# Order of a fused decoder layer's operations, written out by hand, laid out anew on all four engines

## What is computed

```python
x = _layernorm(x + _L0_attn_ref(x, Wq, Wk, Wv, Wo))        # 16 heads of 128, 4 key/value heads, rope, softmax
x = _layernorm(x + _L0_xattn_ref(ctx, ctx, x, filt, D, 8)) # causal long convolution of k*v products, times q
x = _layernorm(x + _L0_ffn_ref(x, W_gate, W_qkv))          # top-1 gated key/value head, causal softmax attention
```

## Time and profile before

| | |
|---|---|
| median of 3 executions | 339.27 us (338.3 to 340.88) |
| profiled execution | 338.36 us, of which the profile's span is 336.5 us |
| PE busy | 312.7 us (93%) |
| DVE busy | 262.9 us (78%) |
| ACT busy | 231.3 us (69%) |
| POOL busy | 204.7 us (61%) |
| granted TensorE clock | 0.994 of full speed |

### The profile page before, as it was taken

How to read it: one execution, slowest core, us unless ns; L and a number is a source line. 1 busy time by engine, 2 the same in 40 slices (tenths; PEclk the granted TensorE clock), 3 DMA queues, 4 the chain that set the end, 5 groups by cost and what they waited for, 6 DMA issues and landing times.

```text
span 336.5 us, 6269 instructions
## 1 busy us (share of the span) xinstructions
PE 312.7 (93%) x2073; PEld 241.0 (72%) x2073; DVE 262.9 (78%) x502; ACT 231.3 (69%) x693; POOL 204.7 (61%) x289
## 2 busy tenths in 40 slices
PE   6889899999989979999999999999999999999982
PEld 2777678888879868878877977877566576656641
DVE  2776986857866884987697499998899899987656
ACT  3679477858858766867685677554477877777781
POOL 0598865737953827694892159995896876802022
PEclk9999999999999999999999999999999999999997
DMA  6940112010020311313000000000000000000001
GB/s 188 348 184 1 63 33 93 1 33 1 16 79 0 95 32 34 93 62 130 7 2 1 0 3 1 2 0 3 0 0 3 2 1 19 0 18 19 16 14 50
DMA packets 5760, 13.87 MB, mean 41 GB/s; under 512 B 864, under 2 KB 3040, under 8 KB 5472
## 3 DMA queue, kind: packets, MB, share of 16 engines
q1 hardware_dynamic: 5456, 13.08, 11.8%
q10 hardware_dynamic: 272, 0.39, 0.4%
HBM read 12.42 MB, written 1.05 MB: 40 GB/s over the span
## 4 chain that ended last, share of the span: by engine, by line
PE 36%; DVE 23%; issue 15%; POOL 14%; ACT 8%; DMA 3%; POOLq 0%; DVEq 0%; ACTq 0%
PE bank L401 5%; DVE q_rope L1607 5%; PE bank L548 5%; PE bank L423 4%; ACT prob L1163 4%; PE bank L438 4%; DVE t_cos L1594 2%; POOL kv L328 2%; PE bank L659 2%; PE bank L617 2%; POOL t_sin L2287 2%; DVE head_lo L1722 2%; PE bank L670 2%; POOL kv L331 2%; ACT rot L1128 2%
## 5 line engine op out<-in xcount | busy, mean ns | idle before, releaser
L2315 POOL TENSOR_TENSOR prob<-prob,rden 128x512 f32<-128x512 f32 x32 | 35.5, 1114 | 49.4 <-DVE rden L1680 49.4
L2287 POOL TENSOR_TENSOR t_sin<-rot,sin 128x512 f32<-128x512 f32 x36 | 47.3, 1324 | 29.8 <-ACT rot L1128 24.0
L1163 ACT ACTIVATE prob<-bank,neg_max 128x128 f32<-128x128 f32 x128 | 45.4, 376 | 14.2 <-DVE neg_max L1673 14.0
L548 PE MATMUL bank<-wo_hi,head_hi 128*128 128x256 f32 x128 | 38.6, 302 | 1.0 <-DVE head_lo L1722 1.0
L1243 ACT ACTIVATE prob<-bank,fneg_max 128x128 f32<-128x128 f32 x128 | 36.8, 383 | 2.3 <-DVE fneg_max L1837 2.2
L2352 POOL TENSOR_TENSOR rstd<-var_eps,half_pow 128x1 f32<-128x1 f32 (+1 forms) x18 | 11.1, 620 | 41.8 <-DVE var_eps L1762 41.0
L401 PE MATMUL bank<-x_hi,w_hi 128*128 128x512 f32 x96 | 33.0, 425 | 3.4 <-DVE w_hi L1641 1.5
L548 PE MATMUL bank<-wo_hi,head_lo 128*128 128x256 f32 x128 | 36.0, 281 | 0.0
L548 PE MATMUL bank<-wo_lo,head_hi 128*128 128x256 f32 x128 | 35.9, 281 | 0.0
L1607 DVE TENSOR_TENSOR q_rope<-t_cos,t_sin 128x512 f32<-128x512 f32 x28 | 33.4, 1214 | 1.8 <-POOL t_sin L2287 1.7
L1127 ACT COPY rot<-bank 64x512 f32<-64x512 f32 x40 | 23.4, 584 | 16.4 <-PE bank L401 13.7
(11 more groups left out here) (132 smaller groups left out, 812.0 us busy)
## 6 DMA issues: line engine op xcount, KB each, us to landing
w_raw<-in_wqkv SPq DMA_DIRECT2D x4, 768.0 KB, 4.3
toep<-in_toep SPq DMA_DIRECT2D x8, 256.0 KB, 3.1
wo_raw<-in_wo SPq DMA_DIRECT2D x4, 512.0 KB, 3.5
x_raw<-in_xt SPq DMA_DIRECT2D x2, 512.0 KB, 5.4
ctxT<-in_ctx SPq DMA_DIRECT2D x1, 1024.0 KB, 4.9
x<-in_x SPq DMA_DIRECT2D x1, 1024.0 KB, 9.0
out<-x SPq DMA_DIRECT2D x8, 128.0 KB, 1.7
wf<-in_wf SPq DMA_DIRECT2D x1, 784.0 KB, 4.3
```

Of the source, the lines that this page charges most:

```text
L548: last = pe.matmul(acc_bank[k // 2][:, (k % 2) * D:(k % 2 + 1) * D], hp[:, k % 2, h * P:(h + 1) * P], wp[:, g % 2, h, :], start=(h + n == ...
L1163: last = act.activation(prob[:, k % 2, h * P:(h + 1) * P], score_bank[k % 2][:, h * P:(h + 1) * P], ACT.Exp, bias=neg_max[:, k % 2, h:h + ...
L2287: pool.tensor_tensor(t_sin[:, par, :].rearrange("p (b t) -> p b t", b=BH), rot[:, par, :].rearrange("p (b t) -> p b t", b=BH), sin[:, :].u ...
L2315: pool.tensor_tensor(own, own, rden[:, k % 2, :].unsqueeze(2).to_broadcast([P, HG, P]), ALU.mult).then_inc(norm_done, 1)
```

## The change

No function is changed and no call is added or taken away; a line with four unused names is added. The lists of calls of TensorE, ScalarE, VectorE and GpSimd are permuted (477 lines out, 478 in). SyncE's list stays as it is. Cut to what the text below speaks of; the list is named ahead of each part by its hunk.

TensorE, the start, units 0 and 1, the entry to the third block, and the end:

```diff
@@ -730,172 +731,172 @@
             front_scores(0, range(0, 3))
+            front_scores(0, range(3, HG))
             v_turn(0)
-            front_scores(0, range(3, HG))
             front_scores(1, range(HG))
             item(0, "K")
             item(0, "Q0")
-            turn(0, 0)
             scores(0, 2)
             scores(0, 3)
+            turn(0, 0)
             item(0, "Q1")
+            item(0, "Q2")
+            values(0, 0)
             turn(0, 1)
-            values(0, 0)
-            item(0, "Q2")
+            conv(0, first_conv_bank, first_conv_done)
             item(0, "Q3")
+            output(0, 0)
+            values(0, 1)
             turn(0, 2)
-            conv(0, first_conv_bank, first_conv_done)
-            values(0, 1)
-            output(0, 0)
             item(0, "C1")
             item(0, "C2")
-            values(0, 2)
             output(0, 1)
             item(0, "C3")
+            values(0, 2)
+            turn(0, 3)
             scores(1, 0)
+            scores(1, 1)
+            values(0, 3)
+            output(0, 2)
             item(0, "C4")
...
             item(1, "Q2")
             item(1, "Q3")
-            turn(1, 2)
-            values(1, 1)
+            scores(1, 3)
+            item(1, "C5")
             output(1, 0)
-            item(1, "C5")
-            output(1, 1)
             item(1, "C6")
             item(1, "C7")
             item(1, "C8")
-            values(1, 2)
-            turn(1, 3)
-            scores(2, 0)
-            scores(2, 1)
+            values(1, 1)
+            turn(1, 2)
             item(1, "C9")
             item(1, "V")
+            turn(1, 3)
             item(2, "K")
             v_turn(2)
+            values(1, 2)
+            scores(2, 0)
...
             output(7, 3)
+            fscores(0, 0)
             x2_turn(1)
-            fscores(0, 0)
...
             fscores(7, 1)
+            fvalues(6, 3)
             fturn(7, 0)
-            fvalues(6, 3)
             fturn(7, 1)
+            y_turn(6)
             last_values(0)
             last_values(1)
             fturn(7, 2)
             fturn(7, 3)
             last_values(2)
-            y_turn(6)
             last_y_turn(0)
```

ScalarE, the start and the end:

```diff
@@ -1264,305 +1265,305 @@
             front_rotate("Q1")
-            split_x(1)
             front_rotate("Q2")
             front_rotate("Q3")
+            split_x(1)
             front_copy_vT()
+            split_wo(0)
             copy_v(0)
-            split_wo(0)
...
             fexps(7, 1)
-            fexps(7, 2)
+            yT_copy(6)
             fprob_copy(7, 0)
             fprob_copy(7, 1)
+            fexps(7, 2)
             fexps(7, 3)
             fprob_copy(7, 2)
-            yT_copy(6)
```

VectorE, the start with unit 0, the entry to the third block, and the end:

```diff
@@ -1889,376 +1890,376 @@
             first_w_high()
+            split_x(0)
             split_w(0, 0)
-            split_x(0)
             split_w(0, 1)
             front_cos_K()
+            front_cos("Q0")
             front_add_K()
-            front_cos("Q0")
             front_cos("Q1")
-            add_skip(0)
             front_cos("Q2")
+            front_cos("Q3")
             split_x(1)
-            front_cos("Q3")
             row_max(0, 0)
             value_low(0)
             row_max(0, 1)
+            front_add()
             invert(0, 0)
-            front_add()
+            add_skip(0)
             invert(0, 1)
             cos_item(0, "K")
             row_max(0, 2)
-            prob_low(0, 0)
-            invert(0, 2)
             cos_item(0, "Q0")
             add_item(0, "K")
+            invert(0, 2)
+            prob_low(0, 0)
+            row_max(0, 3)
             cos_item(0, "Q1")
+            head_low(0, 0)
             prob_low(0, 1)
-            head_low(0, 0)
             add_item(0, "Q0")
...
+            row_max(1, 1)
+            add_skip(1)
+            add_skip(2)
             split_w(1, 0)
...
             mix_norm(0)
+            first_apply(2)
+            prob_copy(7, 1)
             invert(7, 2)
-            second_apply(0)
-            prob_copy(7, 1)
             head_low(7, 0)
             row_max(7, 3)
-            prob_copy(7, 2)
             accumulate(6, 1)
+            second_apply(0)
...
             head_low(7, 3)
+            add_mix(1)
+            set_mask()
             mix_norm(1)
+            accumulate(7, 1)
             second_apply(1)
-            accumulate(7, 1)
...
+            y_invert(6)
             ffn_norm(5)
+            y_scale(6)
             ffn_apply(5)
+            ffn_norm(6)
             last_turn_copy()
-            y_invert(6)
-            y_scale(6)
+            ffn_apply(6)
             last_scale(0)
             last_scale(1)
-            ffn_norm(6)
             ffn_norm(7)
-            ffn_apply(6)
             ffn_apply(7)
```

GpSimd, the start of unit 0's part:

```diff
@@ -2360,91 +2361,91 @@
             normalize(0, 0)
-            normalize(0, 1)
             sin_item(0, "K")
             sin_item(0, "Q0")
+            normalize(0, 1)
+            split_wo(0)
+            sin_item(0, "Q1")
             normalize(0, 2)
-            sin_item(0, "Q1")
-            split_wo(0)
             sin_item(0, "Q2")
             sin_item(0, "Q3")
+            normalize(0, 3)
             pairs(1, range(0, 3))
             pairs(1, range(3, HD))
-            normalize(0, 3)
```

More of the change, by code:

```diff
@@ L810, in _ @@
             turn(2, 3)
-            output(2, 0)
+            scores(3, 0)
             item(2, "C14")
@@ L814, in _ @@
             scores(3, 1)
+            item(3, "K")
+            v_turn(3)
+            output(2, 2)
             scores(3, 2)
@@ L817, in _ @@
             turn(3, 0)
[L818 to L821, removed]
             item(3, "Q0")
-            turn(3, 1)
[L824 to L829, removed]
+            item(3, "Q1")
+            scores(3, 3)
+            item(3, "Q2")
+            item(3, "Q3")
+            values(3, 0)
+            turn(3, 1)
             output(2, 3)
             item(3, "C15")
+            output(3, 0)
             item(3, "C16")
             values(3, 1)
+            turn(3, 2)
             scores(4, 0)
-            output(3, 0)
+            item(3, "C17")
             output(3, 1)
-            item(3, "C17")
             item(3, "C18")
@@ L876, in _ @@
             turn(5, 0)
-            item(5, "K")
+            output(4, 2)
             scores(5, 2)
@@ L881, in _ @@
             values(5, 0)
+            turn(5, 1)
+            output(4, 3)
             item(5, "Q2")
             item(5, "Q3")
-            turn(5, 1)
-            output(4, 3)
+            turn(5, 2)
+            values(5, 1)
+            scores(5, 3)
+            item(5, "C26")
             output(5, 0)
-            scores(5, 3)
+            item(5, "C27")
+            output(5, 1)
             scores(6, 0)
[L889 to L892, removed]
             item(5, "C28")
@@ L1987, in _ @@
             invert(2, 3)
-            head_low(2, 1)
             prob_low(2, 2)
+            accumulate(1, 1)
+            split_w(2, 0)
+            add_skip(4)
             row_max(3, 0)
-            prob_low(2, 3)
-            accumulate(1, 1)
+            row_max(3, 1)
             head_low(2, 2)
             invert(3, 0)
-            row_max(3, 1)
+            value_low(3)
+            prob_low(2, 3)
             row_max(3, 2)
-            split_w(2, 0)
+            cos_item(3, "K")
+            split_w(2, 1)
@@ L1998, in _ @@
+            accumulate(2, 0)
+            add_item(3, "K")
             invert(3, 1)
-            invert(3, 2)
-            value_low(3)
-            split_w(2, 1)
+            cos_item(3, "Q0")
             head_low(2, 3)
+            cos_item(3, "Q1")
             prob_low(3, 0)
-            cos_item(3, "K")
-            cos_item(3, "Q0")
-            prob_low(3, 1)
-            add_item(3, "K")
             add_item(3, "Q0")
-            cos_item(3, "Q1")
-            head_low(3, 0)
-            add_skip(4)
@@ L2034, in _ @@
             cos_item(4, "K")
             add_item(4, "K")
+            cos_item(4, "Q0")
             prob_low(4, 0)
-            cos_item(4, "Q0")
+            cos_item(4, "Q1")
+            accumulate(3, 0)
+            add_skip(6)
             add_item(4, "Q0")
-            invert(4, 1)
-            invert(4, 2)
-            add_skip(5)
-            head_low(4, 0)
-            cos_item(4, "Q1")
             add_item(4, "Q1")
-            add_skip(6)
-            prob_low(4, 1)
             cos_item(4, "Q2")
@@ L2048, in _ @@
             cos_item(4, "Q3")
-            accumulate(3, 1)
-            head_low(4, 1)
-            row_max(4, 3)
-            add_item(4, "Q2")
-            add_item(4, "Q3")
-            prob_low(4, 2)
-            invert(4, 3)
-            row_max(5, 0)
+            head_low(4, 0)
+            add_item(4, "Q2")
+            row_max(4, 3)
+            invert(4, 2)
+            prob_low(4, 1)
+            add_item(4, "Q3")
+            head_low(4, 1)
+            invert(4, 3)
+            prob_low(4, 2)
@@ L2057, in _ @@
+            row_max(5, 0)
```

(10 more changed lines are left out.)

751 lines of the change are left out of this document (373 added, 378 removed).

## The result

The changed kernel took 322.9 us (322.77 to 323.41, 4 runs), before beside it 339.49 us: a ratio of 0.951, interval 0.948 to 0.955. It is 16.6 us faster; 334.0 was forecast, with 330.0 as the low end of the range. The profiled execution took 322.93 us, its span is 321.1; against the profiled execution of before, 338.36 us, that is 15.4 us less.

A forecast was written before the change was run, and what follows sets the result against it. PE, busy 93%, was taken to bound the kernel, with its idle time winnable. Start 2.5, units 0 to 7 2.3 and end 0.5 sum to 5.3 us: 339.27 to 334.0 us, range 330.0 to 339.2.

The forecast's parts named there:

- What bounds it: Whole kernel: PE is 93% busy; in the middle, its 12.5 us of waits on VectorE, late through sums behind GpSimd, are winnable.
- The start, 2.5 us: Start of the kernel: reordering shortens PE's wait for the last head's sine; 3.0 us worked out, 2.5 taken.
- The three parts: Start: earlier x_lo, 0.5 us; ScalarE's cast behind Q2 and Q3, 1.6; x_lo of half 1 behind the cosines, 0.9.
- How many collisions go: Units 0 to 7: the new order avoids 40% of 24.5 us of VectorE's collisions in sums and skip terms, 10 us.
- VectorE is on the chain for 23%, so 10 x 0.23 = 2.3 us: Units 0 to 7: of 10 us saved on VectorE, its chain share of 23% reaches PE, giving 2.3 us.
- Nothing that is moved there shortens it: Third block's steady part: PE is busy 19.78 of 20 us from 300 to 320 us, so reordering gains nothing.
- The end, 0.5 us: End: ffn_norm(6) leaves the last chain, 0.74 us, less 0.24 for later last_turn_copy and fexps(7, 2); net 0.5.
- A: Rival: only start and end gain, VectorE's saved time falls into its idle time; 336.3 us, chance 0.27.
- B: Rival: the wait changes sides, GpSimd's 68 sines and products wait up to 0.65 us each; 342.5 us, chance 0.12.
- The rule of the Trainium skill: VectorE instructions with two SBUF inputs and GpSimd ones reading SBUF exclude each other; a moved sum may merely go ahead.
- C: Rival: waits go with the collisions, half of PE's 12.5 us of waits on VectorE disappears; 330.0 us, chance 0.11.
- The waits that I cost at nothing: Attention: scores(1, 3) with less cover, and add_skip(2) right behind add_skip(1), at most 3.1 us once if cover is gone.

The follow-up runs named there:

- start_only: Kernel before with only the start of all four engine lists, up to the first two score steps, in the new order: 337.0 us.
- long_after: Changed kernel with each full sum made a reduction over t_cos and t_sin in one tensor, one SBUF input, 1.24 us long, no collisions: 328.5 us.
- attn_only: Kernel before with only units 0 to 7 (attention) of all lists in the new order, start and third block old: 328.9 us.
- tail_only: Kernel before with only the end (behind fscores(7, 1) on PE, ffn_apply(4) on VectorE) in the new order: 340.7 us.
- the repair: Changed kernel with last_turn_copy put ahead of ffn_norm(6) on VectorE: 322.85 us.
- early_attn: Kernel before with only units 0 to 2 of attention, up to output(1, 3) and prob_low(2, 2), in the new order: 341.6 us.
- long_attn: Kernel before with units 0 to 7 in the new order and each full sum a 1.24 us reduction with one SBUF input, no collisions: 334.1 us.
- red_before: Kernel before, old order, with all 36 sums made short reductions with one SBUF input, the sine's addition left out, so they can't collide: 327.7 us.
- third_only: Kernel before with only the third block behind output(7, 3) and the end in the new order: 336.9 us.
- third_steady: Kernel before with only the third block behind output(7, 3) in the new order, the end behind fscores(7, 1) old: 337.1 us.
- late_attn: Kernel before with only units 5 to 7 of attention, behind values(5, 0) up to output(7, 3), in the new order: 335.8 us.
- long_before: Kernel before, old order, with each full sum a 1.24 us reduction over t_cos and t_sin in one tensor, no collisions: 337.6 us.
- skip_before: Kernel before, old order, with the 16 skip terms made reductions with one SBUF input, the dcoef term left out, sums unchanged: 337.1 us.

## Why the prediction was right in kind and wrong in size

**What bounds it.** Right: the sums behind GpSimd's operations. Removing their collisions alone, in the old order, gave 11.9 of 16.6 us.

**The start, 2.5 us.** Measured 2.5 us in the median, and part of that agreement is luck. The three parts went as worked out: the third pair of matmuls at 9.13 (9.35 worked out), the last head at 18.30 and 18.56 in the two profiles with the new start (18.5), the `x_lo` of half 1 nearly off the sines. But only 1.8 of the 2.7 us at the last head were left at unit 1, and executions at a mean clock of 0.992 or more differ by 1.5 us (336.84 against 338.34). The rest of the 2.5 us is that 7 of 10 executions of start_only had such a clock and 2 of 13 of before. Whether the new start is the reason for that isn't shown; in long_after, which has it, the clock fell there all the same.

**How many collisions go.** 40% of 24.5 us, 10 us, was forecast. Measured by the groups (K's sums at 9.1 us counted from their own mean): 42.5 + 9.5 - 31.6 - 6.0 = 14.4 us, some 60%. The mean of the q_rope sums, 0.907 us, is in the range that was named. This step was too small by a third.

**The step that failed: "VectorE is on the chain for 23%, so 10 x 0.23 = 2.3 us".** In the old order 64% of the saved time of the sums reached the end and 43% of that of the skip terms. With these rates attention's 10.6 us can be added up: the groups of attn_only have the sums at 31.0 us and the skip terms at 5.9; 42.5 - 31.0 = 11.5 us at 64% is 7.4, 9.5 - 5.9 = 3.6 us at 22 to 43% is 0.8 to 1.5, and 1.7 to 2.4 us are left for the order itself, no more than the 3.5 us that the new attention gives at equal, long sums, of which the skip terms are a part. So the term of the sum that failed is attention's: 2.3 us stood there, 10.6 were measured. The share of one engine in the chain wasn't the price of its time. Why is argued, not shown: the chain names each moment by one engine, but a late sum also holds up the next sine, which waits for the buffer, and that the next sum, so the time that the chain gives to GpSimd and to "issue" may be partly of VectorE's making. All of the chain that wasn't PE was 64% in the old order and 26% in the new, and the sums' measured rates were 64% and 29%; that fits, but the long sums in the new order cost 44% of their time, and the skip terms in the old one at most 43%. So it is no more than a rough guide.

**The third block.** "Nothing that is moved there shortens it" was wrong: 2.5 us in the median, 1.4 at equal clock. I had read the window 300 to 320 us, where PE is busy 19.78 of 20 us, for the whole block; the stretch from 220 to 260 us, where it was busy 19.21 and 19.37 of 20, wasn't looked at by itself.

**The end, 0.5 us.** With the third block the end gave 0.2 us more (336.9 against 337.1), which is within the scatter; alone it lost 1.1. The two terms were those named, `ffn_norm(6)` off the chain and `last_turn_copy` late; in tail_only the latter took more than the 0.24 us put against it, as PE waited 2.55 us for it in place of 0.47. In the whole new order the repair changed nothing, so there the next wait stands right behind.

**The rivals.** A (only start and end, 336.3) is refuted by attention's 10.6 us. B (the wait changes sides): GpSimd's means had to rise by 0.32 us; the sine went from 1.324 to 1.308 us and the product from 1.114 to 1.104. The rule of the Trainium skill that was set against the change (SBUF — State Buffer, "Who interferes with whom") holds for the pair: sums with two SBUF inputs took 0.654 to 2.401 us, those with one 0.676 in the mean. But the sums got 0.3 us shorter in the mean and GpSimd's operations no longer, so they were not merely put ahead of them. C (the waits go with the collisions, 330.0) was the nearest in kind, and still too small by 7 us.

**The waits that I cost at nothing.** `add_skip(2)` behind `add_skip(1)`: VectorE waited 0.3 us in all for skip terms' DMAs. `scores(1, 3)` late: PE has no gap from 40 to 60 us.

## What to carry to other kernels

When one engine does small operations for several others in rings of two buffers, don't price its time by its share of the chain (23% here, where 64% of it counted): measure the rate with a kernel in which that operation is made short and can't collide. The rate holds for that order alone; in the new order it was 29%. Check a new order stage by stage, with cuts at places where every engine has the same steps behind it; one engine's place at a milestone says little if the others' lists are behind. In this kernel a gain at the start went through attention unchanged, while one at the very end was replaced by the next wait. Compare differences of 1 or 2 us between executions of the same granted clock.

## What the runs showed of the hardware that was not expected

A short idle time of TensorE can cost twice. In the profile of early_attn it was busy for 2.00 of 4 us, and then ran 3 us and more at the lower clock level; the granted clock is 1.00 from 84 to 92 and from 96 to 100 us. It need not come so: in the profile of before PE was busy for 2.35 us from 18 to 22 us and the clock stayed at 1.00, while in that of long_attn, which starts in the same order, it was 0.66 from 20 to 24 us. The start has the same thing in some executions and not in others of the same kernel: in the profile of tail_only, whose start is that of before, the pair of matmuls on `x_lo` took longer,

```profile
9.25 1.22 PE L402 MATMUL bank<-x_lo,w_hi 128*128 128x512 f32 x2 [1.33 <-DVE x_lo L1621]
```

against 0.73 us in the earlier trace rows after the same wait of 1.33 us, and the projections behind it were 0.9 us late (52.03 against 51.15). The runs of before fall into groups by their mean granted clock: about 338.3 us at 0.994, 339.5 at 0.989, 340.9 at 0.986 and 341.9 at 0.983, with a few between. A part of what looks like scatter of 1% goes with this; that each group is one such place in the kernel is not shown.

So the median of a few executions mixes two things. The table sets beside it the difference from before among executions with a mean clock of 0.992 or more (before: median 338.34 us, 13 executions; the others 1 to 7, so these are rough, and the mean takes in the idle end too):

| run | by medians, us | at 0.992 or more, us |
|---|---|---|
| red_before | -11.9 | -11.5 |
| start_only | -2.5 | -1.5 |
| attn_only | -10.6 | -10.4 |
| third_only | -2.7 | -2.9 |
| third_steady | -2.5 | -1.4 |
| tail_only | +1.1 | +1.3 |
| early_attn | +2.0 | +1.0 |
| late_attn | -3.9 | -3.4 |
| long_before | -2.1 | -1.5 |
| skip_before | -2.5 | -1.3 |

The large terms stand; the small ones are known to about 1 us. The kernel after had no execution above 0.992; in its profile the clock is at 1.00 up to 312 us, and its 322.93 us are 15.4 below the profiled execution of before, which had no lower clock ahead of its end either.
